# Last stage of a four-stage block: TensorE's expert tiles in a loop of four per round, and tiles made of two 128-row columns

## The reference

```python
logits = x @ gate_w + gate_b                       # x: 4096 tokens x 128, already normalised
probs = jax.nn.softmax(logits, axis=-1)            # over 8 experts
top_w, top_idx = jax.lax.top_k(probs, 2)
top_w = top_w / jnp.sum(top_w, axis=-1, keepdims=True)
combine = jnp.zeros((T, 8)).at[jnp.arange(T)[:, None], top_idx].set(top_w)
h = jax.nn.silu(jnp.einsum('td,edf->tef', x, w1)) * jnp.einsum('td,edf->tef', x, w3)   # f: 512
out_e = jnp.einsum('tef,efd->ted', h, w2)
out = jnp.einsum('ted,te->td', out_e, combine)
x = x + _layernorm(out)
```

## Time and profile before

| | before |
|---|---|
| median of 3 runs | 1427.17 us (1422.79 to 1429.26) |
| profiled execution, and its span | 1431.11 us, 1429.2 us |
| TensorE matmul busy in the span | 1128.2 us, 79% |
| VectorE, ScalarE, GpSimd busy | 1013.2, 786.9, 724.3 us |
| mean granted TensorE clock | 0.903 |
| first expert load to last product of the tiles | 1116.9 to 1383.7 us |

### The profile page before, as it was taken

One profiled execution on the slowest core, in us unless ns is written; L12 is line 12 of the kernel. 1 busy time (PEld: TensorE's weight loads), 2 busy tenths in 40 slices (PEclk: granted clock), 3 DMA queues, 4 the chain that ended last, 5 costly groups with the idle time before them and its releaser, 6 DMA issues. The chain is left out here.

```text
span 1429.2 us, 16931 instructions
## 1 busy us (share of the span) xinstructions
PE 1128.2 (79%) x5006; PEld 560.7 (39%) x5006; DVE 1013.2 (71%) x1416; ACT 786.9 (55%) x1269; POOL 724.3 (51%) x611
## 2 busy tenths in 40 slices
PE   5664789999999988888887979786684678777764
PEld 1221234444444433333333333332243557566563
DVE  4996775665745378999999999999828544444444
ACT  5664545645654468686777768584343333333344
POOL 0112341422312038787878888777621565555554
PEclk8875789999999989999999999998986788898885
DMA  6000000000000001000000000000001111111114
GB/s 207 0 1 0 0 1 1 0 1 0 0 0 1 0 30 30 15 16 15 15 16 15 29 0 0 0 0 1 0 15 45 28 42 37 39 40 39 38 43 168
DMA packets 13850, 33.27 MB, mean 23 GB/s; under 512 B 3568, under 2 KB 3760, under 8 KB 13552
## 3 DMA queue, kind: packets, MB, share of 16 engines
q1 hardware_dynamic: 8784, 22.10, 4.7%
q0 software_dynamic: 4992, 10.23, 2.7%
HBM read 23.01 MB, written 9.31 MB: 23 GB/s over the span
## 5 line engine op out<-in xcount | busy, mean ns | idle before, releaser
L1617 POOL TENSOR_TENSOR prod<-hs,csb 128x1024 f32<-128x1024 f32 x128 | 302.2, 2361 | 181.2 <-DVE hs L1667 179.4
L1667 DVE TENSOR_TENSOR_SCAN hs<-dA,carry,pD 128x512 f32<-128x512 f32 x256 | 313.8, 1268 | 5.5 <-DVE pD L1682 0.8
L1425 PE MATMUL pY<-prod,const 128*128 128x512 f32 x512 | 246.7, 604 | 13.5 <-DVE h L1652 9.3
L1532 ACT ACTIVATE dA<-dt,negA 128x512 f32<-128x512 f32 x256 | 169.9, 715 | 1.4 <-DVE dt L1719 1.4
L2388 DVE SCALAR_TENSOR_TENSOR hid<-pR,silu 128x512 f32<-128x512 f32 x78 | 53.9, 691 | 137.7 <-ACT silu L2099 75.9
L1543 ACT ACTIVATE csb<-pC 128x512 f32<-128x512 f32 x128 | 76.2, 595 | 134.8 <-PE pC L1438 134.6
L1425 PEld LDWEIGHTS pY<-prod,const 128*128 128x128 f32 x512 | 95.7, 192 | 123.9 <-issue 103.7
L2165 POOL DMA_INDIRECT moe_outs<-y,to x78 | 80.5, 1032 | 96.1 <-ACT y L2091 80.1
L2099 ACT ACTIVATE silu<-pR 128x512 f32<-128x512 f32 x78 | 46.5, 596 | 131.8 <-remote 72.6
L2145 POOL DMA_INDIRECT g<-moe_rows,source x78 | 80.8, 1036 | 48.9 <-DVE source L2337 25.8
L1878 PE MATMUL pR<-x,moe_hi 128*128 128x256 f16 x312 | 93.6, 300 | 10.2 <-DVE hid L2388 4.4
(11 more groups left out here) (398 smaller groups left out, 2752.8 us busy)
## 6 DMA issues: line engine op xcount, KB each, us to landing
raw<-moe_w SPq DMA_DIRECT2D x12, 512.0 KB, 3.7
room<-moe_outs SPq DMA_DIRECT2D x8, 512.0 KB, 7.9
X<-xT SPq DMA_DIRECT2D x4, 512.0 KB, 4.5
hidw<-hid_w SPq DMA_DIRECT2D x1, 2048.0 KB, 9.9
moe_rows<-xt SPq DMA_DIRECT2D x8, 256.0 KB, 2.0
outT<-X SPq DMA_DIRECT2D x8, 256.0 KB, 2.0
g<-moe_rows,source POOLq DMA_INDIRECT x78
moe_outs<-y,to POOLq DMA_INDIRECT x78
```

Source lines behind the costliest of these rows:

```text
L1425: last = nc.tensor.matmul(YB[c][:], G.ident, prod[:, slot(b, n), c, :], start=n == 0, stop=n == DST - 1)
L1532: last = nc.scalar.activation(dA[:, slot(b, n), c, :], dt[:, b, c, :], ACT.Exp, scale=negA[:, c, n:n + 1])
L1617: nc.gpsimd.tensor_tensor(prod[:, slot(b, n), :, :], hs[:, slot(b, n), :, :], csb[:, slot(b, n), :, :].to_broadcast([P, CB, N]), ALU.mult)\
L1667: last = nc.vector.tensor_tensor_scan(hs[:, slot(b, n), c, :], dA[:, slot(b, n), c, :], dBu(n, c), carry[:, b, n, c:c + 1], ALU.mult, ALU.add)
```

## The change

An expert's rows are padded to 128, and each of a tile's two columns of 128 rows may belong to another expert. So 8192 pairs need 64 + 7 = 71 columns at most, 36 tiles. `expert` has one number per column, and `up` and `down` compute addresses and load weights for each column `r` apart. `up` has 24 matmuls of 128 columns per unit where it had 12 of 256; `down` keeps 12 of 128. TensorE's stream becomes three written-out steps, a loop of 8 rounds with four steps each, and a written-out end. Waits within the loop compare with a number that depends on the round. A round reloads the expert numbers of three tiles that the previous one knew, since registers aren't carried over. `GR` and `AHEAD` become 4. The wait of `down` on `y_out` is made unconditional by counting two up in advance (`FREE`).

```diff
-    TILES = (PAIRS * P + E * (ROWS - 1)) // ROWS
+    TILES = -(-((PAIRS * P + E * (P - 1)) // P) // 2)
...
-    GRID = B * T // ROWS
-    AHEAD, GR, HR, YR = 6, 8, 4, 4
+    GRID = B * T // P
+    AHEAD, GR, HR, YR = 4, 4, 4, 4
...
-        past = sb("past4", [1, TILES, E])
+        past = sb("past4", [1, COLS, E])
...
-            def up(n, e):
+            def up(k, n, es):
                 i, u = divmod(n, 2)
                 if u == 0:
-                    pe.wait_ge(S["x_in"], i + 1)
+                    pe.wait_ge(S["x_in"], k * GR + (i + 1))
                 if n >= 2:
-                    pe.wait_ge(S["hidden"], n - 1)
+                    pe.wait_ge(S["hidden"], k * (2 * GR) + (n - 1))
                 for h in range(2):
                     for out, at in ((R1, 0), (R3, FFN)):
                         m = slice(at + (2 * u + h) * P, at + (2 * u + h + 1) * P)
-                        last = product(out[:, u, h * ROWS:(h + 1) * ROWS], of_expert(w13_hi, e, m), of_expert(w13_lo, e, m),
-                                       x16[:, i % 2, 0, :], x16[:, i % 2, 1, :], True, True)
+                        for r, e in enumerate(es):
+                            s = slice(r * P, (r + 1) * P)
+                            last = product(out[:, u, h * ROWS + r * P:h * ROWS + (r + 1) * P],
+                                           of_expert(w13_hi, e, m), of_expert(w13_lo, e, m),
+                                           x16[:, i % 2, 0, s], x16[:, i % 2, 1, s], True, True)
                 last.then_inc(S["up"], 1)
...
-                    w_hi, w_lo = of_expert(w2_hi, e, m), of_expert(w2_lo, e, m)
-                    for r in range(2):
+                    for r, e in enumerate(es):
+                        w_hi, w_lo = of_expert(w2_hi, e, m), of_expert(w2_lo, e, m)
...
-            def expert_of(i):
-                return pe.value_load(expert[0:1, i:i + 1], min_val=0, max_val=E - 1)
-
+            def expert_of(k, i):
+                return [pe.value_load(expert[0:1, bass.ds(k * (2 * GR) + c, 1)], min_val=0, max_val=E - 1)
+                        for c in (2 * i, 2 * i + 1)]
+
+
+            def step(k, i, es):
+                es[i + 1] = expert_of(k, i + 1)
+                x_turn(k, i + 1)
+                if 2 * i >= LAG:
+                    down(k, 2 * i - LAG, es[(2 * i - LAG) // 2])
+                up(k, 2 * i + 1, es[i])
+                if 2 * i + 1 >= LAG:
+                    down(k, 2 * i + 1 - LAG, es[(2 * i + 1 - LAG) // 2])
+                up(k, 2 * i + 2, es[i + 1])
+
+            HEAD = (TILES - 1) % GR
             pe.wait_ge(S["expert"], 1)
-            es = {0: expert_of(0)}
-            x_turn(0)
-            for n in range(UNITS):
-                i, u = divmod(n, 2)
-                up(n, es[i])
-                if u == 0 and i + 1 < TILES:
-                    es[i + 1] = expert_of(i + 1)
-                    x_turn(i + 1)
-                if n >= LAG:
-                    down(n - LAG, es[(n - LAG) // 2])
-            for n in range(UNITS - LAG, UNITS):
-                down(n, es[n // 2])
+            es = {0: expert_of(0, 0)}
+            x_turn(0, 0)
+            up(0, 0, es[0])
+            for i in range(HEAD):
+                step(0, i, es)
+            with pe.Fori(0, (TILES - 1) // GR) as k:
+                es = {i: expert_of(k, i) for i in range(HEAD - 2, HEAD + 1)}
+                for i in range(HEAD, HEAD + GR):
+                    step(k, i, es)
+            es = {i: expert_of(0, i) for i in range(TILES - 3, TILES)}
+            down(0, UNITS - 2 - LAG, es[(UNITS - 2 - LAG) // 2])
+            up(0, UNITS - 1, es[TILES - 1])
+            for n in range(UNITS - 1 - LAG, UNITS):
+                down(0, n, es[n // 2])
```

More of the change, by code:

```diff
@@ L1743, in phase_moe @@
     QP = PAIRS // QUARTERS
-    GRID = B * T // ROWS
-    AHEAD, GR, HR, YR = 6, 8, 4, 4
+    GRID = B * T // P
+    AHEAD, GR, HR, YR = 4, 4, 4, 4
     SOON, LATE = 16, COLS - 16
     LAG = 3
+    FREE = 2
     BIG = 1e30
@@ L1799, in phase_moe @@
         low_h = sb("low_h4", [P, PAIRS], F16)
-        past = sb("past4", [1, TILES, E])
-        expert_f = sb("expert_f4", [1, TILES])
-        expert = sb("expert4", [1, TILES], I32)
+        past = sb("past4", [1, COLS, E])
+        expert_f = sb("expert_f4", [1, COLS])
+        expert = sb("expert4", [1, COLS], I32)
         row_f = sb("row_f4", [P, COLS])
@@ L1845, in phase_moe @@
                  "past expert_f expert hot_col hot_part hot_pair hot_low listed row_f empty second from_f to source "
-                 "gathered0 gathered1 gathered2 gathered3 gathered4 gathered5 gathered6 gathered7 scattered0 scattered1 scattered2 scattered3 x_turned x_in up silus hidden hid_high hid_low down y_out "
+                 "gathered0 gathered1 gathered2 gathered3 scattered0 scattered1 scattered2 scattered3 x_turned x_in up silus hidden hid_high hid_low down y_out "
                  "back0 back1 back2 back3 back4 back5 back6 back7 summed minus squaredC weighted logC rstdC scale scaledC turnedC addedC stored").split()
@@ L1952, in _, with x_turn @@
             last.then_inc(S["listed"], 1)
-            def x_turn(i):
-                pe.wait_ge(S[f"gathered{i % GR}"], 32 * (i // GR + 1))
+            def x_turn(k, i):
+                pe.wait_ge(S[f"gathered{i % GR}"], k * 32 + 32 * (i // GR + 1))
                 if i >= 2:
-                    pe.wait_ge(S["x_in"], i - 1)
+                    pe.wait_ge(S["x_in"], k * GR + (i - 1))
                 for w in range(2):
@@ L1976, in up, with down @@
                         m = slice(at + (2 * u + h) * P, at + (2 * u + h + 1) * P)
-                        last = product(out[:, u, h * ROWS:(h + 1) * ROWS], of_expert(w13_hi, e, m), of_expert(w13_lo, e, m),
-                                       x16[:, i % 2, 0, :], x16[:, i % 2, 1, :], True, True)
+                        for r, e in enumerate(es):
[3 more added lines that the diff above has]
+                                           x16[:, i % 2, 0, s], x16[:, i % 2, 1, s], True, True)
                 last.then_inc(S["up"], 1)
-            def down(n, e):
+            def down(k, n, es):
                 i, u = divmod(n, 2)
-                pe.wait_ge(S["hid_low"], n + 1)
-                if u == 0 and i >= 2:
-                    pe.wait_ge(S["y_out"], i - 1)
+                pe.wait_ge(S["hid_low"], k * (2 * GR) + (n + 1))
+                if u == 0:
+                    pe.wait_ge(S["y_out"], k * GR + (i - 1 + FREE))
                 for h in range(2):
                     m = slice((2 * u + h) * P, (2 * u + h + 1) * P)
-                    w_hi, w_lo = of_expert(w2_hi, e, m), of_expert(w2_lo, e, m)
-                    for r in range(2):
+                    for r, e in enumerate(es):
+                        w_hi, w_lo = of_expert(w2_hi, e, m), of_expert(w2_lo, e, m)
                         out = Y[:, i % 2, r * P:(r + 1) * P]
@@ L2162, in _ @@
                 pool.wait_ge(S["to"], lists(i))
-                pool.wait_ge(S["y_out"], i + 1)
+                pool.wait_ge(S["y_out"], i + 1 + FREE)
                 for r in range(2):
@@ L2186, in _ @@
             nc.vector.memset(keep[:, :, :], 1.0)
-            nc.vector.memset(one8[:, :], 1.0)
+            nc.vector.memset(one8[:, :], 1.0).then_inc(S["y_out"], FREE)
             nc.vector.tensor_copy(ident16[:, :], G.ident).then_inc(S["lanes_in"], 1)
@@ L2266, in _ @@
             steps = lane_f[:, 0:GRID].unsqueeze(1).to_broadcast([P, E, GRID])
-            nc.vector.scalar_tensor_tensor(out=grid[:, :, :], in0=steps, scalar=float(ROWS),
+            nc.vector.scalar_tensor_tensor(out=grid[:, :, :], in0=steps, scalar=float(P),
                                            in1=counts.unsqueeze(2).to_broadcast([P, E, GRID]),
@@ L2280, in _ @@
             nc.vector.scalar_tensor_tensor(out=place[:, :, :], in0=tiles_from[:, :].unsqueeze(2).to_broadcast([P, E, CHUNKS]),
-                                           scalar=float(ROWS), in1=rank, op0=ALU.mult, op1=ALU.add)\
+                                           scalar=float(P), in1=rank, op0=ALU.mult, op1=ALU.add)\
               .then_inc(S["place"], 1)
@@ L2355, in _ @@
             targets(listed_soon, slice(0, SOON), 0)
-            nc.vector.tensor_tensor(past[:, :, :], tiles_to[0:1, :].unsqueeze(1).to_broadcast([1, TILES, E]),
-                                    lane_f[0:1, 0:TILES].unsqueeze(2).to_broadcast([1, TILES, E]), ALU.is_le)\
+            nc.vector.tensor_tensor(past[:, :, :], tiles_to[0:1, :].unsqueeze(1).to_broadcast([1, COLS, E]),
+                                    lane_f[0:1, 0:COLS].unsqueeze(2).to_broadcast([1, COLS, E]), ALU.is_le)\
               .then_inc(S["past"], 1)
```

## The result

The changed kernel took 1493.8 us (median of 4 runs, 1492.8 to 1495.0) against 1427.2 us for the kernel before (1422.8 to 1429.3): a ratio of 1.048, 95% interval 1.046 to 1.050. It is slower, by 66.6 us; 1527 us was predicted, so the direction and the limit were right and the size was 33 us too high. The experiments showed two things behind these numbers. The 30 us of code patches in the sum do not exist. And the kernel before is itself 60 us faster on three of the four chips of the experiments, 1365 us. The changed kernel is not: on the one of these three where it ran too, it took 1493 us as here, and the ratio was 1.094.

What follows compares the result with a forecast made beforehand. TensorE was taken as bound by its array, plus ten waits for code; after the change, by its sequencer. Tiles: 288 + 34 + 30 + 10 + 5 = 367 us, 100 more, so 1527 us predicted, range 1455 to 1570.

Steps and rivals of the forecast that it cites:

- code patches: TensorE in the tiles: waits for its own written-out code, 3.5 left in place of ten, 30 us in all.
- the sum: Tiles: 288 + 34 + 30 + 10 + 5 = 367 us in place of 266.8, 100 us more.
- The sequencer as the limit: TensorE's tiles: 24 register pairs at 0.24 us, 5.8 us, over the array's 4.26; loads in full; chance 0.73.
- The round: TensorE's loop: 36.0 us for four tiles, 8 rounds 288 us, plus 1.2 us a round for the clock, 10 us.
- Head and end: TensorE's written-out tiles 34 us; ScalarE's waits 2 us, first turn and `take_x` 2 us, last result 1 us.
- GpSimd's issues: GpSimd in the tiles: four DMA issues of 1.03 us, well under a tile of 7.7 us or more; nothing gained.
- Packets: TensorE's instruction queue: 14 or 15 packets fewer, none from the second round on.
- code fetched anew: Rival, TensorE's loop: body of 870 instructions may not stay, 104 us more, 1631 us; chance 0.05.
- overlapping loads: Rival, expert loads in the loop: they overlap or are covered, 1459 us, partly covered up to 1490; chance 0.12.
- hidden sequencer: Rival, TensorE's tiles: the array stays the limit, 188 us, 79 us less, 1348 us; chance 0.07.
- main case: TensorE's tiles: sequencer as the limit with loads in full, own range 1490 to 1565 us; chance 0.73.
- computed addresses at no cost: Expert loads in the loop: low side of the main case's range, 13 us less.

Runs made afterwards that it cites:

- e5: Changed kernel with one fixed address for the low halves of the weights, so one register instruction per matmul group in place of two: 1410.6 us.
- e4: Changed kernel without the six loads at a round's start that read three known tiles' expert numbers again: 1459.5 us, ratio 1.024.
- e9: Kernel before, unchanged, run again on a third chip: 1364.8 us.
- e1: Kernel before with only TensorE's loop of four tiles per round, tiles of 256 rows as before, nothing split: 1432.6 us, ratio 1.005.
- e2: Changed kernel with its split tiles written out, without the loop, 72 loads in place of 126: 1442.2 us, ratio 1.012 to the kernel before.
- e3: Kernel before, gathering only a tile's first column and using it for both, so half of the rows are wrong: 1374.0 us, ratio 0.964.

## Why the prediction came out as it did

- **The sequencer as the limit: right.** Most pairs of register instructions of `up` are 0.24 us apart as forecast, and e5 takes half of the register instructions away and gets 82 us. The array's 4.26 us a tile and the other engines' waits decide nothing, as said.
- **The round: 36.7 us for 36.0 + 1.2.** Its parts hold too: a load in a row 0.77 us (0.77 forecast), 0.71 us by e4; tiles within a round 7.8 to 8.1 us apart (7.7 forecast); 6.5 us without a matmul at the start (6 forecast); behind them the 1.2 GHz level. Rounds: 293.7 us for 288 + 10.
- **Head and end:** 1142.2 - 1116.1 and 1447.8 - 1435.9 are 26.1 + 11.9 = 38 us, for the 34 written out and 5 at the ends.
- **Code patches: wrong.** The step that failed is "so the patches are TensorE waiting for its own code", and with it the term 3.5 x 8.7 = 30 us. Measured: none. The sum without the term is 337 us for 331.7 measured; with it, 367. The inference rested on a count that fitted (20 packets, ten patches) and on the word "issue", which names no cause. It could have been refuted in the trace before: I took "one patch for about two packets" without looking whether a packet comes in each patch, or what the other engines do in one. GpSimd's timeline beside the earlier trace rows was one view left out. The other is the queues in the window of each patch: queue 8 has a packet in two of the ten. In that of the earlier trace rows, 1151.7 to 1158.9 us, there is one queue alone, which carries the gathers and scatters:

```profile
q0 software_dynamic: 174, 0.37, 18.1%
```

- **GpSimd's issues: priced too low, without harm to the sum.** The prediction takes "four DMA issues of 1.03 us a tile", which is their busy time; from one to the next it is 1.3 us, 5.2 us a tile. That is still under the 7.8 us and more of a tile after. But it is over the 4.2 us at which the prediction had the tiles before running if there were no patches: without them (e9) they take 201.3 us and not 163.
- **Packets:** 26 for 40, none on queue 8 from the second round to the end of the loop: right. A body of 870 instructions stays. The Trainium skill (Runtime: NRT & Kernel Launch, section on instruction fetch mechanics) would have each taken branch fetch again where the target is out of its two-page window; the trace shows no such packet and a branch of 0.21 us, and the measurement decides. The same section of the Trainium skill gives TensorE's instruction memory as 2048 instructions, which the prediction passed over; with that figure the trace agrees, since the body of 870 fits. The rival of code fetched anew, like the overlapping loads and the hidden sequencer, is out.
- **The sum:** 64.9 us more in the tiles for 100 forecast; the missing patches are 30 of these 35 us, small terms the other 5. The time is inside the range by luck as far as the patches go. The range allowed 13 us less for them, not 30. 1493.8 us still lies above the 1490 us at which the main case's own range begins, because that range also left room for a full clock and for computed addresses at no cost, and neither came.

The part of the forecast that no view of one profile could give is the chip. The change costs 66 us against the kernel before with its patches, and 128 us against the same kernel on a chip without them. The loop takes few patches away: e1 keeps eight of ten. The split takes all (e2), as the tile grows from 4.2 to 7.8 us, above GpSimd's 5.2, so on a chip with patches it hides part of its own price, and on another it doesn't. Of the 266.8 us before, 201.3 us are the tiles as GpSimd bounds them, and the other 65 us are what the chip with patches adds.

**Open.** What a patch is. It was seen on one chip of the four and in the first profile; it goes with GpSimd issuing through two tiles without a pause (e1, e3: yes; e2 and the changed kernel, where GpSimd waits for results: no), and does not come on three other chips under the same load. A rival that no run was made for: TensorE's own dense running, since in e2 and the changed kernel TensorE has gaps too. The trace before speaks against it. Behind the last gather GpSimd has two issues a tile and pauses, TensorE stays dense, and no patch comes in 28 us, where the others come 14 to 21 us behind the one before (span, busy and count of TensorE's matmuls, clock, DMA share, GB/s):

```profile
1355.40:1383.60 28.20, 26.98 (x317) 0.94 0.15 34
```

Whether the number of indirect DMAs or GpSimd's being busy counts was not told apart: both runs meant for it came to chips without patches. That the profiler makes it is unlikely, since the profiled and the timed runs agree (1431 and 1427 us), but was not tested.

## What to carry to other kernels

Before a change splits matmuls that take their address from a register, count the register instructions per matmul group and compare with the group's time on the array: at 0.12 us each, and 0.7 us for a value load, they set the pace here as soon as the array had less than 0.24 us of work for a pair. A loop whose rounds reload registers pays each load in full when the sequencer is the limit (34 us here). And an "issue" wait is a question, not an answer: look at what every other engine does in it, and, before a stall is put into a sum, whether it is there on another chip.

## What was not expected of the hardware

- One program, two times, by the chip: 1425.6 us on one, 1366.4, 1364.8 and 1365.9 us on three others, each within some 0.6% in itself. The changed kernel took 1493.8 and 1492.6 us, and the written-out tiles with fixed low addresses 1354.3 and 1354.8 us: these two, which have no patches, took the same time on both chips that they ran on.
- In a patch TensorE starts single instructions some 0.7 us apart (1261.94, 1262.60, 1263.34 in e1) with nothing on its instruction queue.
- A taken branch costs 0.21 us, and a loop body of about 870 instructions runs without a packet of code from the second round on.
- GpSimd spends 1.3 us on each indirect DMA, 1.0 us of it busy; four a tile bound a stage whose matmuls take 4.2 us.
